# Last block's token attention: keys placed by DMA instead of a GpSimd masked copy, and the engines' lists in a new order

## What is computed

```python
def _mha(x, y, wq, wk, wv, li1_w, li1_b, lnx_g, lnx_b, lny_g, lny_b, ln3_g, ln3_b, li2_w, li2_b, li3_w, li3_b, causal):
    xn = _ln(x, lnx_g, lnx_b)
    yn = _ln(y, lny_g, lny_b)
    q = jnp.einsum('bsc,hcd->bhsd', xn, wq)
    k = jnp.einsum('btc,hcd->bhtd', yn, wk)
    v = jnp.einsum('btc,hcd->bhtd', yn, wv)
    a = jax.nn.softmax(jnp.einsum('bhsd,bhtd->bhst', q, k) * D ** (-0.5), axis=-1)
    if causal:
        s, t = (a.shape[-2], a.shape[-1])
        mask = (jnp.arange(t)[None, :] > jnp.arange(s)[:, None]).astype(a.dtype)
        a = a * mask
    o = jnp.einsum('bhst,bhtd->bhsd', a, v)
    o = o.transpose(0, 2, 1, 3).reshape(x.shape[0], x.shape[1], H * D)
    x_out = x + o @ li1_w + li1_b
...
x = _ln(xx, ln1_g, ln1_b)
x = x + _mha(x, x, a1_wq, ..., causal=True)
```

## Time and profile before

| | |
|---|---|
| median of 3 runs | 5404.17 us (5402.6 to 5416.16) |
| the profiled execution | 5395.1 us, span 5393.3 us |
| mean granted TensorE clock | 0.925 of full speed |
| busy shares of the span | PE 87%, Vector 70%, Scalar 54%, GpSimd 40% |
| the stage `l3a` | about 3227 to 4027 us of the span |

### The profile page before, as it was taken

The page is one execution under the profiler, slowest core; times in us unless marked ns, Lnnn a source line. Parts: engine busy times, 40 slices in busy tenths (PEclk is TensorE's granted clock), DMA queues, the critical chain, the costliest instruction groups (busy, mean ns, idle before and its releaser), DMA issues. The chain is left out here.

```text
span 5393.3 us, 135149 instructions
## 1 busy us (share of the span) xinstructions
PE 4696.6 (87%) x42171; PEld 3414.4 (63%) x42171; DVE 3795.1 (70%) x9705; ACT 2899.9 (54%) x7246; POOL 2176.5 (40%) x3095
## 2 busy tenths in 40 slices
PE   7998998999952699688989988999988899998898
PEld 4665668888852466455556666666666677776554
DVE  6776867777766333577767768888877899997444
ACT  4665765555530233344455548888873555554354
POOL 5552001011127100566633338888878333333200
PEclk9998999999975899777799999999999999999888
DMA  1004200000011344100000000000000000000000
GB/s 41 7 10 189 89 1 6 5 5 5 5 57 43 110 138 136 46 21 21 29 11 1 0 6 1 0 0 0 0 7 1 3 2 2 2 2 7 0 14 18
DMA packets 108951, 140.36 MB, mean 26 GB/s; under 512 B 35832, under 2 KB 83256, under 8 KB 103996
## 3 DMA queue, kind: packets, MB, share of 16 engines
q1 hardware_dynamic: 100544, 120.88, 6.6%
q0 software_dynamic: 8192, 16.79, 1.0%
HBM read 47.44 MB, written 58.72 MB: 20 GB/s over the span
## 5 line engine op out<-in xcount | busy, mean ns | idle before, releaser
L285 ACT ACTIVATE l3a_probs<-l3a_scores,l3a_mx 128x128 f32<-128x128 f32 x1024 | 363.5, 402 | 0.4 <-issue 0.4
L2273 POOL TENSOR_TENSOR l3a_probs<-l3a_probs,l3a_later 128x512 f32<-128x512 f32 x256 | 325.8, 1273 | 82.9 <-ACT l3a_probs L285 82.1
L191 POOL TENSOR_TENSOR l1x_ve<-l1x_mv,eps 128x1 f32<-128x1 f32 x64 | 12.3, 192 | 648.8 <-DVE l1x_mv L183 648.8
L1757 POOL TENSOR_TENSOR l2f_hid<-l2f_prod,l2f_route 128x512 f32<-128x512 f32 x128 | 152.3, 1195 | 254.3 <-DVE l2f_prod L1904 244.4
L2321 PE MATMUL l3a_scores<-l3a_keys,l3a_qT 128*128 128x512 f32 x512 | 251.2, 600 | 3.6 <-POOL l3a_keys L2259 3.6
L285 ACT ACTIVATION_READ_ACCUMULATOR l3a_probs<-l3a_scores,l3a_mx 128x1 f32 x1024 | 248.1, 242 | 0.0
L2259 POOL TENSOR_TENSOR l3a_keys<-l3a_kT,head 128x2048 f32<-128x2048 f32 x64 | 230.5, 3602 | 2.9 <-ACT l3a_kT L2390 2.9
L1643 PE MATMUL l1e_h<-l1e_xhi,l1f_parts 128*128 128x512 f16 x640 | 204.2, 380 | 9.7 <-DVE l1e_gated L1701 8.2
L310 ACT ACTIVATE l3c_hiT<-l3c_turned 77x512 f16<-77x512 f32 x256 | 150.4, 588 | 106.7 <-PE l3c_po L331 104.2
L2259 POOL TENSOR_TENSOR l3c_keys<-l3c_kT,head 128x1232 f32<-128x1232 f32 x64 | 144.1, 2252 | 156.5 <-ACT l3c_kT L2390 156.5
L317 DVE SCALAR_TENSOR_TENSOR l1x_loT<-l1x_turned,l1x_hiT 77x512 f16<-77x512 f32 x256 | 168.9, 679 | 49.6 <-ACT l1x_hiT L310 49.5
(11 more groups left out here) (587 smaller groups left out, 17280.5 us busy)
## 6 DMA issues: line engine op xcount, KB each, us to landing
l_rows<-l0f_zeros SPq DMA_DIRECT2D x34, 1024.0 KB, 27.1
l1f_parts<-l1f_split SPq DMA_DIRECT2D x40, 512.0 KB, 3.6
l1e_x_in<-l_rows SPq DMA_DIRECT2D x40, 256.0 KB, 2.8
l1f_down<-l1f_w SPq DMA_DIRECT2D x40, 256.0 KB, 2.4
l_rows<-l1e_y_out SPq DMA_DIRECT2D x40, 256.0 KB, 2.7
l1f_w<-in_L_W SPq DMA_DIRECT2D x16, 256.0 KB, 3.6
out_x<-x_res SPq DMA_DIRECT2D x16, 256.0 KB, 2.0
x_res<-in_x SPq DMA_DIRECT2D x1, 3840.0 KB, 12.2
```

The source lines that it names most:

```text
L285: last = act.activation(self.probs[it.par][:, h, :], self.view(c)[:, h - a, :], ACT.Exp, bias=self.mx[it.par][:, h:h + 1], scale=-1.0, acc ...
L1757: pool.tensor_tensor(hid[k % 2][:, :].rearrange("p (e m) -> p e m", m=M), prod[k % 2][:, :].rearrange("p (e m) -> p e m", m=M), rt.w[it.pa ...
L2273: pool.tensor_tensor(v, v, later[:, :].unsqueeze(1).to_broadcast([P, 4, T]), ALU.mult).then_inc(s_masked, 1)
```

## The change

`keys` is cleared once at the stage's start by two GpSimd memsets. After that, `spread` is gone from GpSimd's list. In its place SyncE waits, batch by batch, for `kT` (and for the scores of the batch two before, which read the same buffer) and issues four DMAs, SBUF to SBUF, one per head of a group: 32 rows of `kT` (4 runs of 512 bytes each, 64 KB in all) to the same rows of the head's columns in `keys`. The zeros around them stay. `score` now waits for all four on `s_placed` of its parity, and `fetch_k` waits until the DMAs that read the old `kT` have landed. The loads of the next stage's weights come behind the loop in SyncE's queue. The `first=False` attention (`l3c`) keeps the GpSimd copy. All four engines' lists of the stage have a new order and new lags:

```diff
+        s_placed, s_clear = st.sem2("s_placed"), st.sem("s_clear")
...
+                else:
+                    sp.wait_ge(s_clear, 2)
+
+                    def place_keys(it):
+
+                        p = it.par
+                        sp.wait_ge(s_kT, nth(it))
+                        if (due := nth(it, 4, ago=2)) is not None:
+                            sp.wait_ge(sm.s_scores, due)
+                        for h in range(G4):
+                            rows = slice(h * D, (h + 1) * D)
+                            sp.dma_start(keys[p][rows, :, h, :], kT[p][rows, :, :]).then_inc(s_placed[p], 16)
+
+                    skewed(sp, g.B, [(place_keys, 0)], 4)
                 load_ahead(sp, g)
...
                 if first:
+                    for k in keys:
+                        pool.memset(k[:, :, :, :], 0.0).then_inc(s_clear, 1)
                     pool.memset(later[:, :], 1.0).then_inc(s_mask, 1)
...
-                steps = {"spread": (spread, 3), "deviation3": (lambda it: n3.inverse_deviation(pool, it), 2 if first else 1)}
+                steps = {"deviation3": (lambda it: n3.inverse_deviation(pool, it), 2 if first else 1)}
...
-                    names = ("drop2:5 deviation2:1 drop3:5 drop0:4 deviation1:0 drop1:4 deviation3:1 spread:3")
+                    names = ("deviation1:1 deviation2:2 drop2:5 drop3:5 drop0:4 drop1:4 deviation3:2")
...
                 def score(it, c):
-                    pe.wait_ge(s_keys, nth(it))
+                    if first:
+                        pe.wait_ge(s_placed[it.par], loads(it, G4))
+                    else:
+                        pe.wait_ge(s_keys, nth(it))
...
-                    names = ("score2:3 output:5 queries:2 turn_p2:4 score3:3 keys:2 weigh0:4 weigh1:4 turn_p3:4 values:2 weigh2:4 "
-                             "weigh3:4 turn_p0:3 turn_p1:3 turn_o:4 score0:2 turn:1 score1:2")
+                    names = ("turn_p0:3 weigh2:4 weigh3:4 turn_p1:3 score0:2 score1:2 turn:1 score2:2 turn_o:4 queries:1 score3:2 "
+                             "output:4 keys:1 turn_p2:3 weigh0:3 weigh1:3 turn_p3:3 values:1")
...
                 def fetch_k(it):
                     act.wait_ge(s_k, nth(it))
-                    if (due := nth(it, ago=2)) is not None:
+                    if first:
+                        if not isinstance(it.b, int) or it.b >= 2:
+                            act.wait_ge(s_placed[it.par], it.half * (16 * G4))
+                    elif (due := nth(it, ago=2)) is not None:
                         act.wait_ge(s_keys, due)
...
-                    names = ("fetch_p3:6 exp2:5 fetch_v:4 fetch_p0:5 exp3:5 fetch_o:6 fetch_x:3 exp0:4 exp1:4 fetch_q:3 "
-                             "fetch_p1:5 fetch_k:3 fetch_p2:5")
+                    names = ("fetch_p3:5 exp2:4 fetch_v:3 exp3:4 fetch_p0:4 fetch_x:2 exp0:3 fetch_o:5 fetch_q:2 fetch_p1:4 "
+                             "exp1:3 fetch_k:2 fetch_p2:4")
...
-                    names = ("remainder3:6 stats1:0 divide:6 values:4 hat:2 remainder0:5 maximum0:4 maximum1:4 stats3:1 add:6 "
-                             "maximum2:4 remainder1:5 stats2:0 maximum3:4 remainder2:5")
+                    names = ("stats1:0 remainder2:6 remainder3:6 maximum3:5 hat:3 divide:6 values:4 maximum0:4 maximum1:4 "
+                             "remainder0:5 stats3:2 maximum2:4 add:6 remainder1:5 stats2:1")
```

More of the change, by code:

```diff
@@ L2278, in _ @@
                                  deviation2=(lambda it: n2.inverse_deviation(pool, it), 1), **numbered("drop", drop_earlier, 4, 4))
-                    names = ("drop2:5 deviation2:1 drop3:5 drop0:4 deviation1:0 drop1:4 deviation3:1 spread:3")
+                    names = ("deviation1:1 deviation2:2 drop2:5 drop3:5 drop0:4 drop1:4 deviation3:2")
                 else:
-                    steps.update(deviation_y=(lambda it: ny.inverse_deviation(pool, it), 2), begin_y=(begin_y, 4))
+                    steps.update(deviation_y=(lambda it: ny.inverse_deviation(pool, it), 2), begin_y=(begin_y, 4), spread=(spread, 3))
                     names = "deviation_y spread deviation3 begin_y"
```

## The result

The changed kernel is slower: **5418.72 us median** (5402.2 to 5437.55, 20 runs) beside 5402.11 (5388.14 to 5427.49, 20 runs) for the one before in the same job, a ratio of **1.003, 95% interval 1.0018 to 1.0043**. I had forecast 5382 us, 0.4% faster. The time lies inside the range that I gave, but the kernel moved the other way.

The account below looks back on a forecast made before the run. Vector was taken as the bound; 0.41 us a batch over 58 batches (-23.8), memsets +3.3 and drain -2 sum to -22.5: 5395.1 becomes 5372.6, and with the median 9.1 higher, 5382 us; range 5360 to 5428.

Parts of the forecast that it names:

- Vector's waits as the gain: Stage, steady batches: Vector's own work is 11.30 of 12.06 us, so at most 0.76 us a batch to gain.
- rival 3: Stage: all Vector's waits for GpSimd vanish, 11.30 us a batch, 5361 us; chance 0.10 for it or near it.
- The walk, T + 11.65: Steady batch, from one start of PE's xh transpose (T) to the next: 11.65 us, 0.41 less than 12.06.
- hidden by 0.2 us: Key DMAs: keys placed at T + 9.75, needed by score0 at T + 9.93, so no delay to the batch.
- The gap at `stats1`: Vector, steady batch: the "issue" gap after a drain, taken at about 0.2 us.
- Fill and drain: Stage's start and end: memsets ahead of GpSimd's first norm add 3.3 us, one lag less on PE takes 2 off.
- Rival 1: Stage: drop1 starts ahead of stats2's scaling, mean 12.04 us a batch, 5404 us, no change; chance 0.24 with late DMAs.
- Rival 2: Stage: stats3's sum writing z also waits behind drop0, +0.64 us a batch, 5443 us if each batch; chance 0.22.

Follow-up runs that it names:

- a2_old_lists: The changed kernel's four DMAs and two memsets with the four engine lists of the kernel before; ratio 1.0005 to the kernel before, pace 12.049 us a batch.
- e7_before_cut: The kernel before, with Vector's loop boundary moved behind the drain at the end of stats2; ratio 1.0042 to the kernel before, pace 12.189 us.
- a1_rotate: The changed kernel with Vector's loop boundary moved between the first two maxima, same instruction order; ratio 1.0068 to the kernel before, pace 12.544 us.
- h1_deviations: The changed kernel with GpSimd's deviation1 moved behind drop3 and deviation3 between drop0 and drop1; ratio 0.9998 to the kernel before, pace 11.975 us.
- c3_both: The changed kernel with hat moved ahead of remainder 3 and stats1 behind maximum 3 on Vector; ratio 1.0010 to the kernel before, pace 11.936 us.
- c1_stats1: The changed kernel with stats1 moved behind remainder 3 and hat left in place; ratio 1.0028 to the kernel before, pace 12.132 us.

## Why the prediction was wrong

**Vector's waits as the gain: wrong.** This step failed first. I took 12.06 less Vector's own 11.30 as what could be gained. a2_old_lists removes 0.24 us of `hat`'s wait and gains nothing, since Vector then waits 0.25 us for scores; only at another place, behind `stats2`, did a delay of Vector come through whole (e7_before_cut). In the changed kernel the walk behind `drop2` and the DMAs' chain lie within 0.16 us of each other. The freed GpSimd time was worth nothing by itself, as I said, and rival 3 is out.

**The walk, T + 11.65: the mechanism right, three terms too small.** `stats2`'s scaling against `drop1`: T + 5.34 beside T + 5.47 (turn at 3496.17), forecast 5.52 and 5.49. My own figures had `drop1` ahead by 0.03 us, and the forecast took the scaling to win: that it did so was luck. In the trace it was ahead by 0.11 us or more in all batches but one of the fill (held for 1.29 us at 3292.7), and a lead of 0.09 was not enough (a1_rotate's section). `drop2`: forecast T + 8.75, by ScalarE's chain alone. It starts at T + 9.05 to 9.09, since the three deviations, which the list puts behind `drop1`, are not over before. **That is the mis-sized step**, 0.3 us. h1_deviations, where `drop2` starts at T + 8.81 to 8.86, undoes most of it. I had counted what GpSimd's instructions cost in sum and not where they stood in its queue. From `values` to the next `turn` I had 0.73 us; it is 0.82 and 0.90, because Tensor comes to `turn` later than Vector is ready. Together: 10.35 + 0.9 + 0.85 = 12.1, the measured terms of the pace.

**The DMAs, "hidden by 0.2 us": the room was not there.** Forecast 5.85 + 3.9 + 1.72 = 11.47 us as their floor. `kT` was ready at T + 5.85 in the batch from 3508.32 (3514.17). From there to `score0` (3518.38) it took 4.2 us, as the issues are 0.64 apart and not 0.59, with 0.15 to 0.2 to wake Tensor; and from `score0` to `turn` 1.97, not 1.72. These make up the 12.03 us of that batch. Of the 1.97, 0.15 are a wait of `turn` for `vlo`, since the scores need 1.82 (c3_both's rows); so the DMAs alone would have given 11.88, and in this batch `hat` behind `drop2` set the rest. In the batch of 12.15 us `turn` did not wait for `vlo`: `kT` was ready at T + 6.02, the keys 4.09 later, and `score0` 0.23 and `turn` 1.82 behind that. There the DMAs' chain alone was the pace, with `kT` 0.17 us later than in c3_both (T + 5.85). With `hat` out of the way (c3_both) it still takes 11.86 and 11.99, not 11.47. The landing, 2.0 us, was right: by the Trainium skill (DMA: Bandwidth & Descriptors, Anatomy of one DMA, whose fit is of DMAs issued by GpSimd) 64 KB would add 0.15 us, an estimate, to a fixed cost of about 2.0; the trace shows 2.0 in all. The term that was too small is the issue, four in a row on one queue, and the wake behind the landing, 0.13 to 0.23 us, was missing.

**The gap at `stats1`, 0.80 us in place of 0.2: missed, and worth nothing here.** c1_stats1 takes it off the chain at no gain. In the old list, where no slack covers it, such a gap does count (e7_before_cut).

**Fill and drain: memsets right (+3.3, as forecast), the rest wrong.** I took 2 us off and found 8.1 + 1.0 + 1.6 more. I had walked the steady state only, and there the placing has 3.9 us of other work beside it. In the fill it has almost none. That is the larger part of the loss: of 16.3 us, 3.3 are memsets, 2.2 the steady pace, 8.1 the fill (5.9 without the batch at the lowered clock), 2.6 the end.

**Rival 1** gave "same" by a lost meeting, which did not occur; a1_rotate shows its price, 0.45 us a batch beside the 0.39 I had. **Rival 2**'s second meeting, `z` with `drop0`, did not occur either: `z` starts 0.28 us ahead (3510.62 beside 3510.90) and lasts 0.29. What came out, 0.3% slower, was in the range but in none of the rivals.

## What to carry to other kernels

Before a saving on one engine is priced, the instructions behind the one that others wait for are to be walked in each queue in their order, GpSimd's small ones too: 2.3 us of them stood ahead of the mask step that mattered. A copy replaced by DMAs trades engine time for latency: four issues at 0.64 and 2.0 to land can nearly hide in a full pipeline and, in this order of steps, not in the batches that fill it, so a fill needs a walk of its own. Where several limits lie within 0.2 us, removing one shows only the next: no edit alone made the stage shorter than before, and three at once (order, issue queues, clearing) gained 0.6%.

## What the runs showed of the hardware

A scaling from SBUF to SBUF that started 0.01 us beside GpSimd's mask step lost 1.04 us, one that started 0.13 us ahead nothing. Such a meeting had no middle in these traces: up to 0.09 us ahead all 35 were held, from 0.10 on none of 608. By the rule of the Trainium skill (SBUF — State Buffer, two separate sides) whoever starts first holds the shared ports. The 3.23 us above agree; the 35, recorded as first and still held, agree only if the two engines' recorded starts may be 0.1 us off against each other, which no run tests.

Vector's instructions that read PSUM were not held: 193 of them started inside a key copy in the kernel before, and they lasted 0.68 to 0.69 us. A loop's boundary behind a drain cost Vector 0.33 to 0.45 us more than the same place without it, and nothing visible between two long instructions. And where Tensor waited 0.6 to 0.9 us longer than in its usual batch, some of those batches took 1.6 us and more too long, with a granted clock of 0.56 and 0.87 of full speed in the two stretches behind the wait (a1_rotate), or 0.64 and 0.79 (the changed kernel).
